# A graph network of two RGCN and two GAT layers on one core: unread products on TensorE before each slot's product

## The chip, the core and the metric

The kernel runs on one core of a Trainium2 chip. The time is the device time of one execution in microseconds. A core has TensorE (PE, matmuls from SBUF into PSUM banks), VectorE (DVE), ScalarE (ACT), GpSimd (POOL, which here issues all gathers) and SyncE (SP, DMA and semaphores). They run on their own and wait for each other by semaphores.

## The reference, cut to what matters

There are 6,250 nodes of 128 features and 100,000 edges, sorted by their destination `dst`. Two RGCN layers are followed by two GAT layers:

```
# RGCN, twice
agg = segment_sum(h[src], dst * 16 + rel)            # one sum per node and relation
out = relu(einsum('nri,rio->no', agg, W) + h @ loop_w + bias)
# GAT, twice, 4 heads
e     = leaky_relu(al_s[src] + al_d[dst], 0.2)
alpha = exp(e - segment_max(e, dst)[dst]) / segment_sum(...)[dst]
out   = segment_sum(alpha * xw[src], dst) + b
```

What costs is the sum over edges: a row per edge is gathered from a table in HBM and added to the row of its destination.

## The kernel before, in words

**Slots.** The edges lie in 784 tiles (`NT`) of 128 edges. The nodes lie in 49 windows of 128. A slot is a tile together with a window that it touches; there are 832 (`NS`). For each slot VectorE builds a 128 x 128 selection matrix `Sr` (1 where an edge's destination is a node of the window), TensorE multiplies it with the gathered tile `Gr` into a PSUM bank `B`, and VectorE adds the bank to the window's rows in `AC`. All of this is float32; TensorE takes such a product in two passes, so the profile shows two records for each.

**Stages.** After a first part (tables, layer norm, the table of the first RGCN layer) come four slot stages: RGCN layer 1 and 2 (`L` 0 and 1 in `tensor`, gathers on line 1872, slot products on line 1650, additions on line 852), and GAT layer 1 and 2 (`gat_tensor`, gathers on line 1889, slot products on line 1770, additions on line 1033). During the RGCN stages a turn (`onward_tensor`, `outward_tensor`) is woven in every 9 slots (`EVERY`): it takes a finished window, transposes it (line 1528, copied by VectorE on line 524) and multiplies it for the next layer (lines 1550 and 1552, or 1569). During the GAT stages `prep` is woven in: for the next chunk of 32 slots it transposes and multiplies in bf16 (lines 1705, 1719) and works out the weights of the edges with VectorE and ScalarE. The GAT chunks number 26.

**What orders the slots.** The order on each engine is written out by hand. The RGCN slot product waits for its bank, freed by the addition of three or four slots ago (`slot_add`; the banks are `RGCN_BANKS`, three in the first layer, four in the second), and for its tile: SyncE counts the landed gathers into `landed` (line 1914), and a register holds how many the slot needs. GpSimd gathers ahead, at most so far that tile `sn` waits for slot `sn - 16` (line 1871); in the GAT stages for slot `s - 96` (line 1888), and there a whole chunk's gathers are awaited by ScalarE in `prep`, not by TensorE. The GAT slot product waits for its bank alone (`gat_add`, three banks), and at a chunk's first slot for the weighing.

Of the kernel before, what the change touches and what calls it, by code (L numbers as in the profile page):

```python
# [37 lines left out]
HW = NW // 2  # L38
SLOW_STORES = (24, 30)
RGCN_BANKS = ((0, 1, 2), (0, 1, 2, 7))  # L40
PARAMS = 224
XC = 16
SG = 8
# [43 lines left out]
def build(nc, I, out, dbg=None):  # L87
# [7 lines left out]
    with ctx:  # L95
# [195 lines left out]
        def sel(s):  # L291
            return Sr[:, (s % SR) * P:(s % SR + 1) * P]
# [1262 lines left out]
        def outward_tensor(e, k):  # L1555
# [14 lines left out]
            yield  # L1570
            yield

        def tensor(e):
            pregs = [registers(e, f"t{k}", 16) for k in range(2)]
            kregs = [registers(e, f"tile{k}", 16) for k in range(2)]
            def mix(l, k):
                half, c = k // 2, k % 2
                if k == 0:
                    e.wait_ge(mixv.sem, mixv.at(f"wdg{l}"))
                    e.wait_ge(mix_par[l], 32)  # L1580
                if l:
                    e.wait_ge(mixa, 4 + k)
                e.matmul(B[7 if l else MIX_BANK[k]][:, :], wdg[l][:, half * P:(half + 1) * P], bas[l][:, c * 512:(c + 1) * 512],
                         start=True, stop=True).then_inc(mixp, 1)
            for k in range(4):
                mix(0, k)
            e.wait_ge(flagv.sem, flagv.at("sum"))
            e.wait_ge(const, CONST["ones"])
            e.matmul(B[1][0:1, 0:1], small[:, 0:1], ones[0:RF, 0:1], start=True, stop=True).then_inc(flagp, 1)

            tables = tables_tensor(e)
            early = False
            e.wait_ge(const, CONST["ident"])
            for w in range(-1, NW):
                if w + 1 < NW:
                    turned(e, w + 1)
                if w < 0:
                    continue
                e.wait_ge(hT_made, w + 1)
                for k in range(5):  # L1600
                    if w:
                        if k % 2 == 0 and k < 4:
                            e.wait_ge(row_a, 2 * (w - 1) + k // 2 + 1)
                        else:
                            e.wait_ge(row_v, 3 * (w - 1) + {1: 1, 3: 2, 4: 3}[k])
                    elif k == 0:
                        e.wait_ge(mixa, 4)
                        e.wait_ge(flagv.sem, flagv.at("flag"))
                    if k < 4:
                        if w == 0 and k == 0:  # L1610
                            e.wait_ge(wall_sem[0], 16)
                        e.matmul(B[k][:, :], hT[:, w % 2, :], wl[0][:, k * 512:(k + 1) * 512], start=True, stop=True).then_inc(row_mm, 1)  # L1612
                    else:
                        if w == 0:
                            e.wait_ge(first_params, 32)
                        e.matmul(B[k][:, 0:P], hT[:, w % 2, :], lw[0][:, :], start=True, stop=True).then_inc(row_mm, 1)
                if 8 <= w < 12:
                    if w == 8:
                        e.wait_ge(tv.sem, tv.at("rs"))
                    mix(1, w - 8)  # L1620
                if w >= 1 and not early:
                    early = next(tables) == "early"

            for L in range(2):
                turn = iter(())
                banks = RGCN_BANKS[L]

                def start(k):
                    return onward_tensor(e, k) if L == 0 else outward_tensor(e, k)
                if L == 0:  # L1630
                    e.wait_ge(params, PARAMS)
                    e.wait_ge(row_a, 2 * NW)
                    e.wait_ge(row_v, 3 * NW)
                    e.wait_ge(ta.sem, ta.at("oft1"))
                else:
                    e.wait_ge(rest_done, 1)
                for s in range(-LOOK, NS + LAG):
                    if 0 <= s < NS:
                        if s % 16 == 0:
                            e.reg_load(pregs[s % 32 // 16], OFT[0:1, s:s + 16])  # L1640
                            e.reg_load(kregs[s % 32 // 16], TIX[:, s:s + 16])

                        if s >= len(banks):
                            e.wait_ge(slot_add, L * NS + s - len(banks) + 1)
                        else:
                            e.wait_ge(built_v, L * NS + s + 1)

                        e.wait_ge(landed[L], kregs[s % 32 // 16][s % 16])
                        o = off(e, pregs[s % 32 // 16][s % 16], (TG - 1) * P)
                        e.matmul(B[banks[s % len(banks)]][:, 0:P], selr(s), Gr[:, bass.ds(o, P)], start=True, stop=True).then_inc(slot_mm, 1)  # L1650
                    sa = s - LAG
                    if sa >= 0:
                        if L == 0 and sa % 16 == 8:
                            next(tables, None)
                        k = (sa + 1 - FIRST) // EVERY
                        if sa + 1 >= FIRST and (sa + 1 - FIRST) % EVERY == 0 and k < NK:
                            finish(turn)
                            turn = start(k)
                    next(turn, None)
                finish(turn)  # L1660
                if L == 0:
                    finish(tables)
                turns = turns_of(NK, start)
                if L == 0:
                    for _ in range(2):
                        for x in turns:
                            next(x)
                    for x in turns:
                        finish(x)
                    rest(e, rest_tensor, "rt")  # L1670
                else:
                    for _ in zip(*turns):
                        pass
                    rest(e, rest2_tensor, "r2t")
            for L in range(2):
                gat_tensor(e, L, pregs)

        def gat_tensor(e, L, pregs):
# [79 lines left out]
            for c in range(NC):  # L1758
                gen = prep(c + 1) if c + 1 < NC else iter(())
                for i in range(CH):  # L1760
                    s = c * CH + i


                    if i == 0:
                        e.wait_ge(wei_v, L * (4 * NC - 3) + 4 * c + 1)
                    if c + 1 == NC and i in (8, 16, 24):
                        e.wait_ge(wei_g, 3 * L + i // 8)
                    if s >= 3:
                        e.wait_ge(gat_add, L * NS + s - 2)
                    e.matmul(B[s % 3][:, 0:CW], sel(s), Gr[:, (s % GR) * CW:(s % GR + 1) * CW], start=True, stop=True).then_inc(gat_mm, 1)  # L1770
                    if i < 12 or (i >= 14 and i % 2 == 0):
                        next(gen, None)
# [247 lines left out]
```

## Time and profile before

| | |
|---|---|
| median of 3 runs | 5546.97 us (5546.96 to 5551.64) |
| the profiled execution, its own time | 5593.81 us |
| its span in the trace | 5592.0 us |
| granted TensorE clock, mean | 0.604 |
| busy share of the span | PE 56%, weight loads 41%, DVE 46%, ACT 19%, POOL 57% |
| slot products | 1,664 on line 1650, 1,664 on line 1770, two records each |

A record of PE is one matmul pass; its start is measured, its end is modelled. PEclk is the clock that TensorE was granted, as a share of 2.4 GHz: 1.0 is 2.4 GHz and 0.5 is 1.2 GHz. An idle time is followed by an arrow and by what ended it; "issue" means nothing that the profile shows, "remote" a releaser that it could not name.

### The profile page before, as it was taken

How to read it: one execution, taken by the hardware profiler on the slowest of the kernel's cores; microseconds unless marked ns; L12 is line 12 of the kernel's file. 1: busy time of each engine (PE TensorE's matmuls, PEld its weight loads, DVE VectorE, ACT ScalarE, POOL GpSimd, SP SyncE). 2: the span in 40 equal slices, each digit the busy share in tenths (PEclk: the TensorE clock that was granted, in tenths of full speed). 3: DMA queues.
4: the chain of work that ended last, by engine and by line, in shares of the span. 5: the costliest groups of instructions: out<-in, count | busy, mean ns of one | idle time of the engine just before them, and what ended most of it. 6: DMA issues, size and time to landing. Idle time of an engine off the chain costs nothing.

```text
span 5592.0 us, 63654 instructions
## 1 busy us (share of the span) xinstructions
PE 3147.6 (56%) x12887; PEld 2272.1 (41%) x12887; DVE 2561.5 (46%) x9589; ACT 1064.3 (19%) x2505; POOL 3194.9 (57%) x3310
## 2 busy tenths in 40 slices
PE   7946666676734444444415555655651555555555
PEld 3434333343423333333314444444540444444444
DVE  6433333333333443444515555555571555555557
ACT  3301111121200000000102222222230222222223
POOL 0166666666266666666466666666526666666651
PEclk9957777777855555555555555555565555555556
DMA  6513333333322222222122222222102222222221
GB/s 238 228 44 111 124 121 118 118 119 123 115 71 53 55 54 54 55 54 56 35 48 45 45 45 45 45 45 45 39 26 49 46 44 45 45 45 45 45 43 47
DMA packets 168746, 395.78 MB, mean 71 GB/s; under 512 B 57590, under 2 KB 92468, under 8 KB 151092
## 3 DMA queue, kind: packets, MB, share of 16 engines
q0 software_dynamic: 103872, 215.70, 16.8%
q10 hardware_dynamic: 37968, 103.60, 4.8%
q1 hardware_dynamic: 26532, 72.39, 3.5%
q8 instruction: 126, 2.06, 0.2%
q14 instruction: 248, 2.03, 0.1%
HBM read 230.11 MB, written 161.35 MB: 70 GB/s over the span
## 4 chain that ended last, share of the span: by engine, by line
PE 34%; issue 22%; another core or an unknown queue 21%; DVE 13%; ACT 3%; POOL 2%; DVEq 2%; DMA 1%; SPq 1%; ACTq 0%; POOLq 0%
PE B L1770 9%; PE B L1650 8%; PE B L1550 6%; DVE AC L1033 3%; PE B L1612 3%; DVE AC L852 3%; PE B L1705 2%; PE B L1719 2%; ACT hold L1376 1%; POOL Gr L1889 1%; DVE Sr L937 1%; DVEq L308 1%; POOL Gr L1872 1%; DVE Sr L840 1%
## 5 line engine op out<-in xcount | busy, mean ns | idle before, releaser
L1889 POOL DMA_INDIRECT Gr<-Gtab,SRC x1664 | 1617.4, 972 | 1010.6 <-issue 471.4
L1872 POOL DMA_INDIRECT Gr<-Ttab,GID x1568 | 1501.8, 958 | 1045.6 <-issue 413.4
L1650 PE MATMUL B<-Gr,Sr 128*128 x3328 | 916.8, 402 | 723.7 <-issue 381.3
L1770 PE MATMUL B<-Gr,Sr 128*128 128x136 f32 x3328 | 1059.8, 462 | 402.2 <-DVE AC L1033 187.8
L1650 PEld LDWEIGHTS B<-Gr,Sr 128*128 128x128 f32 x3328 | 742.0, 279 | 1104.2 <-issue 1100.0
L1033 DVE TENSOR_TENSOR AC<-AC,B 128x136 f32 x1664 | 486.9, 293 | 1135.1 <-PE B L1770 470.8
L1770 PEld LDWEIGHTS B<-Gr,Sr 128*128 128x128 f32 x3328 | 786.4, 304 | 520.5 <-issue 243.6
L852 DVE TENSOR_TENSOR AC<-AC,B 128x128 f32 x1664 | 476.3, 286 | 937.8 <-remote 400.2
L1550 PE MATMUL B<-XW,hT 128*128 128x512 f32 x672 | 474.5, 798 | 90.3 <-ACT Sr L1202 32.9
L1705 PE MATMUL B<-identb,hold 128*128 128x128 bf16 x1664 | 251.9, 305 | 464.3 <-ACT hold L1376 259.5
L840 DVE TENSOR_SCALAR Sr<-iota,DL 128x128 f32<-128x128 f32 x1664 | 494.3, 299 | 15.8 <-issue 10.9
L1368 ACT CAST hold<-Sr 128x512 bf16<-128x512 f32 x416 | 257.6, 619 | 977.3 <-remote 500.1
L1705 PEld LDWEIGHTS B<-identb,hold 128*128 128x128 bf16 x1664 | 181.3, 138 | 524.5 <-ACT hold L1376 279.5
L937 DVE TENSOR_SCALAR Sr<-iota,DL 128x128 f32<-128x128 f32 x1664 | 373.8, 300 | 19.3 <-issue 18.9
L1202 ACT COPY Sr<-B 128x512 f32<-128x512 f32 x336 | 195.0, 585 | 648.2 <-PE B L1550 396.9
L1376 ACT COPY hold<-B 128x512 bf16<-128x512 bf16 x416 | 240.3, 584 | 147.7 <-PE B L1719 80.1
L1013 DVE TENSOR_TENSOR Gr<-Gr,B 128x1024 f32<-128x1024 f32 x202 | 245.2, 1214 | 3.4 <-issue 3.4
L1719 PE MATMUL B<-A,hold 128*128 x1664 | 163.2, 186 | 97.3 <-issue 44.4
L1719 PEld LDWEIGHTS B<-A,hold 128*128 128x128 bf16 x1664 | 148.1, 119 | 146.7 <-issue 131.7
L524 DVE COPY hT<-B 128x128 f32<-128x128 f32 x217 | 62.5, 289 | 309.2 <-remote 157.7
L1550 PEld LDWEIGHTS B<-XW,hT 128*128 128x128 f32 x672 | 136.8, 252 | 114.6 <-issue 41.7
L1612 PE MATMUL B<-XW,hT 128*128 128x512 f32 x392 | 179.0, 600 | 6.4 <-DVE hT L524 6.4
(275 smaller groups left out, 2358.2 us busy)
## 6 DMA issues: line engine op xcount, KB each, us to landing
Ttab<-Sr ACTq DMA_DIRECT2D x84, 1024.0 KB
Ttab<-Sr SPq DMA_DIRECT2D x51, 1024.0 KB
Gr<-Gtab,SRC POOLq DMA_INDIRECT x1664
Gr<-Ttab,GID POOLq DMA_INDIRECT x1568
Gtab<-Gr ACTq DMA_DIRECT2D x84, 66.0 KB
X1D<-Gr ACTq DMA_DIRECT2D x84, 64.0 KB
Gtab<-XW SPq DMA_DIRECT2D x7, 462.0 KB, 3.7
out<-Sr SPq DMA_DIRECT2D x12, 256.0 KB
```

What stands on the lines that cost most here:

```text
L840: e.tensor_scalar(out=selr(sn), in0=iota[:, :], scalar1=DL[:, sn:sn + 1], scalar2=None, op0=ALU.is_equal).then_inc(built_v, 1)
L852: e.tensor_tensor(a, a, B[RGCN_BANKS[L][sa % len(RGCN_BANKS[L])]][:, 0:P], ALU.add).then_inc(slot_add, 1)
L937: e.tensor_scalar(out=sel(s), in0=iota[:, :], scalar1=DL[:, s:s + 1], scalar2=None, op0=ALU.is_equal).then_inc(sel_made, 1)
L1033: e.tensor_tensor(a, a, B[s % 3][:, 0:CW], ALU.add).then_inc(gat_add, 1)
L1550: e.matmul(B[bk][:, :], hT[:, u % 2, :], wl[1][:, i * 512:(i + 1) * 512], start=True, stop=True).then_inc(row_mm, 1)
L1612: e.matmul(B[k][:, :], hT[:, w % 2, :], wl[0][:, k * 512:(k + 1) * 512], start=True, stop=True).then_inc(row_mm, 1)
L1650: e.matmul(B[banks[s % len(banks)]][:, 0:P], selr(s), Gr[:, bass.ds(o, P)], start=True, stop=True).then_inc(slot_mm, 1)
L1705: mm = e.transpose(bt[:, j * P:(j + 1) * P], sbf[:, g % 2, j * P:(j + 1) * P], identb[:, :])
L1719: mm = e.matmul(B[5][:, 12 * m:12 * m + 12], sts[:, g % 2, j * P:(j + 1) * P], A3[:, bass.ds(off(e, regs[m % 16], 12 * NW), 12)], start=Tr ...
L1770: e.matmul(B[s % 3][:, 0:CW], sel(s), Gr[:, (s % GR) * CW:(s % GR + 1) * CW], start=True, stop=True).then_inc(gat_mm, 1)
L1872: e.indirect_dma_start(out=Gr[:, (sn + 1) % TG * P:((sn + 1) % TG + 1) * P], out_offset=None, in_=Tt[L][:, :], in_offset=bass.IndirectOffs ...
L1889: e.indirect_dma_start(out=Gr[:, (s % GR) * CW:(s % GR) * CW + 132], out_offset=None, in_=T2[L][0:NPAD][:, :], in_offset=bass.IndirectOffs ...
```

## The change

Before each slot's product TensorE computes further products into the same bank: the bf16 identity as weight, the same identity read four times over as the moving side, so 128 x 512 elements of output. Nobody reads them, since the slot's product starts the bank anew. There is one for each slot of the first RGCN stage and three in the second, not in the last 40 slots (`CALM`), and two in both GAT stages, not in the last chunk. They stand behind the wait for the bank, and in the RGCN stages ahead of the wait for the tile. They signal nothing. The first RGCN stage also waits once for the constant `identb`.

```diff
+RGCN_BUSY, GAT_BUSY, CALM = (1, 3), 2, 40
...
+        def keep_busy(e, bank, n):
+
+            for _ in range(n):
+                e.matmul(B[bank][:, :].rearrange("p (k n) -> p k n", n=P), identb[:, :], identb[:, :].unsqueeze(1).to_broadcast([P, 4, P]),
+                         start=True, stop=True)
+
...
                 if L == 0:
+                    e.wait_ge(const, CONST["identb"])
                     e.wait_ge(params, PARAMS)
...
                             e.wait_ge(built_v, L * NS + s + 1)
+                        if s < NS - CALM:
+                            keep_busy(e, banks[s % len(banks)], RGCN_BUSY[L])
 
                         e.wait_ge(landed[L], kregs[s % 32 // 16][s % 16])
...
                     if s >= 3:
                         e.wait_ge(gat_add, L * NS + s - 2)
+                    if c + 1 < NC:
+                        keep_busy(e, s % 3, GAT_BUSY)
                     e.matmul(B[s % 3][:, 0:CW], sel(s), Gr[:, (s % GR) * CW:(s % GR + 1) * CW], start=True, stop=True).then_inc(gat_mm, 1)
```

On TensorE in the second RGCN stage, two slots stood like this before (L308 is the register instruction that carries the waits, L1650 the slot's product):

```order
L308 ISA [waits landed1,slot_added]
L1650 MATMUL B<-Gr,Sr 128x128
L1528 MATMUL B<-ident,hn 128x128 [waits hT_made,hn_made]
L308 ISA [waits landed1,slot_added]
L1650 MATMUL B<-Gr,Sr 128x128
```

and stand like this now (L1577 is the new product, L1660 the slot's, L309 the former L308, L1529 the former L1528):

```order
L1660 MATMUL B<-Gr,Sr 128x128
L1529 MATMUL B<-ident,hn 128x128 [waits hT_made,hn_made]
L1577 MATMUL B<-identb 128x512 [waits slot_added]
L1577 MATMUL B<-identb 128x512 x2
L309 ISA [waits landed1]
L1660 MATMUL B<-Gr,Sr 128x128
```

The wait for the bank has moved from the slot's own register instruction to the first of the three new products, and the wait for the tile stands behind all three.

On TensorE in the middle of a GAT chunk before (L1719 belongs to the preparation of the next chunk):

```order
L1719 MATMUL B<-A,hold 128x12
L1770 MATMUL B<-Gr,Sr 128x136 [waits gat_added]
L308 ISA [waits prep_scalar]
L1719 MATMUL B<-A,hold 128x12
L308 ISA
```

and now (L1729 is the former L1719, L1782 the former L1770):

```order
L1729 MATMUL B<-A,hold 128x12
L1577 MATMUL B<-identb 128x512 [waits gat_added]
L1577 MATMUL B<-identb 128x512
L1782 MATMUL B<-Gr,Sr 128x136
L309 ISA [waits prep_scalar]
L1729 MATMUL B<-A,hold 128x12
```

Two new products now stand between the preparation's products and the slot's, and they take over the wait for the bank.

## Rows read from the trace of the kernel before

**Rows 1.** The page: TensorE's granted clock in 40 slices, tenths of 2.4 GHz

```profile
PEclk9957777777855555555555555555565555555556
```

**Rows 2.** Stretches: length; busy (records) PE, PEld, DVE, ACT, POOL; clock, DMA share, GB/s

```profile
0.00:240.00 240.00, 204.51 (x607) 98.48 (x607) 136.63 (x384) 82.93 (x161) 19.93 (x40) 0.96 0.63 246
...
300.00:1440.00 1140.00, 750.38 (x2357) 450.65 (x2356) 414.05 (x1658) 198.20 (x380) 719.97 (x752) 0.74 0.34 112
1570.00:2700.00 1130.00, 505.02 (x1731) 394.15 (x1731) 452.03 (x2041) 85.01 (x298) 725.39 (x759) 0.53 0.21 53
2860.00:4030.00 1170.00, 658.54 (x3293) 530.35 (x3293) 587.44 (x2159) 263.69 (x646) 736.85 (x765) 0.53 0.20 45
4280.00:5440.00 1160.00, 658.53 (x3285) 530.71 (x3285) 587.23 (x2162) 261.55 (x642) 725.10 (x760) 0.53 0.21 45
1453.00:1523.00 70.00, 56.19 (x199) 33.30 (x199) 31.41 (x128) 18.55 (x35) 0.00 (x0) 0.85 0.24 99
2703.00:2752.00 49.00, 36.94 (x142) 30.20 (x141) 34.77 (x161) 7.53 (x26) 1.27 (x2) 0.57 0.13 24
5441.00:5523.00 82.00, 62.95 (x332) 51.36 (x332) 53.38 (x195) 21.64 (x54) 5.91 (x4) 0.67 0.02 2
```

**Rows 3.** The additions alone in those stretches, L852 then L1033 (x counts slots)

```profile
300.00:1440.00 1140.00, 215.18 (x750) 0.74 0.34 112
1570.00:2700.00 1130.00, 216.47 (x758) 0.53 0.21 53
...
1453.00:1523.00 70.00, 17.68 (x62) 0.85 0.24 99
2703.00:2752.00 49.00, 17.02 (x60) 0.57 0.13 24
...
4280.00:5440.00 1160.00, 215.21 (x736) 0.53 0.21 45
...
5441.00:5523.00 82.00, 27.01 (x92) 0.67 0.02 2
```

**Rows 4.** Timeline of 16 us in RGCN layer 2: start, us, what

```profile
1858.70 0.28 PE L1528 MATMUL B<-ident,hn 128*128 128x128 f32 x1
...
1859.76 0.95 POOL L1872 DMA_INDIRECT Gr<-Ttab,GID  x1 [0.30 <-issue]
...
1872.09 0.29 DVE L524 COPY hT<-B 128x128 f32<-128x128 f32 x1 [11.24 <-remote]
1872.44 0.82 PE L1569 MATMUL B<-wx,hT 128*128 128x136 f32 x2 [13.11 <-DVE hT L524]
```

**Rows 5.** Gather lines L1872, then L1889: what ended GpSimd's idle time

```profile
  remote: 223.6, 109
  PE B L1650: 211.9, 221
...
  PE B L1770: 248.5, 255
  remote: 230.9, 104
```

**Rows 6.** RGCN slot products: durations (min/median/max), and idle ended by SyncE

```profile
L1650 PE MATMUL B<-Gr,Sr x3328: 272/421/583, 263.9 to 2751.7; 128*128 x196
...
  SPq L1914: 48.6, 12
```

**Rows 7.** Timeline at a change of clock, end of GAT layer 2

```profile
5472.90 0.50 PE L1770 MATMUL B<-Gr,Sr 128*128 128x136 f32 x2 [0.46 <-DVE AC L1033]
5473.35 0.40 PE L1705 MATMUL B<-identb,hold 128*128 128x128 bf16 x4
5474.52 0.82 PE L1770 MATMUL B<-Gr,Sr 128*128 128x136 f32 x2 [0.78 <-DVE AC L1033]
5475.13 0.63 PE L1705 MATMUL B<-identb,hold 128*128 128x128 bf16 x4
```

**Rows 8.** The bf16 transposes of GAT layer 2

```profile
L1705 PE MATMUL B<-identb,hold x732: 216/314/314, 4295.5 to 5437.2; 128*128 128x128 bf16 x183
```

## The prediction

> **What bounds the kernel now.** I read the page first. TensorE's matmuls are busy for 56% of the span and GpSimd for 57% (the table of the profile above), neither of them full, and the line of granted clocks stands at 5 tenths from the 15th slice on, against 9 at the start [rows 1]. So from about 1,560 us on TensorE runs at 1.2 GHz, and this is what the change aims at.
>
> Next the table of stretches, cut where the four slot stages are in steady state (gathers running) and where their gathers have ended [rows 2], and the same stretches for the two lines of VectorE that add one slot each, which count the slots [rows 3]. Dividing gives us per slot. First RGCN stage: 1140/750 = 1.52. Second: 1130/758 = 1.49. The GAT stages: 1170/736 = 1.59 and 1160/736 = 1.58 (736 in both). In the tails without gathers the same work takes 70/62 = 1.13, 49/60 = 0.82 and, at the end of the last stage, 82/92 = 0.89; I take the GAT layer before it for the same.
>
> Is it the gathers, then, that set the pace? Each takes GpSimd 0.95 us and 0.30 us of issue, 1.26 us from start to start [rows 4], less than 1.49 to 1.59. GpSimd itself waits, and for TensorE: the two gather lines waited 212 + 249 us for the slot products and 224 + 231 us for releasers without a name, which at these lines can only be earlier slots or earlier gathers; 915 us in all [rows 5]. Seen from TensorE, the wait for a landed tile (SyncE's line 1914) ended only 49 us of idle time before the RGCN slot products [rows 6]. Tiles are there early; TensorE is late. That is the first warning for this change: the time in which TensorE waits **for a tile** is next to nothing.
>
> What is TensorE late with? By the stretches its matmuls are busy 1.00, 0.67, 0.89 and 0.89 us per slot, and the rest is 0.52, 0.82, 0.70 and 0.68 us. In the tails the rest is only 0.22 (1.13 - 56.19/62), 0.20 and 0.21 us. The timeline shows what the rest is made of: products that have been issued and are taken note of much later. A transpose (L1528) of 0.28 us starts at 1858.70, the copy that waits for it starts at 1872.09, and in these 13 us TensorE starts nothing, while gathers go on every 1.26 us [rows 4]. I call such a stretch a hold. The trace does not tell what makes one; it shows that they are long where gathers run and TensorE is sparse, and nearly absent in the tails.
>
> **The change part by part.** (1) One wait for `identb` before the first RGCN stage. The first slot product starts at 264 us [rows 6], long after GpSimd has made its constants: nothing.
>
> (2) Products: 792 slots x 1, 792 x 3, and 2 x 25 chunks x 32 slots x 2 = 3,200; 6,368 in all. No row shows this product, so it is bounded. It streams 512 bf16 columns over a bf16 weight, as many as four of L1705's. A train of four of these took 0.63 us in the cold clock and 0.40 in the warm one [rows 7]; one alone lasts up to 0.31 and at least 0.22 [rows 8]. So start to start (0.63 - 0.31)/3 = 0.107 and (0.40 - 0.22)/3 = 0.06, and a product is 0.43 us cold and 0.24 warm. The upper bounds are the trains themselves, 0.63 and 0.40. I take 0.43 and 0.24.
>
> (3) The clock. In the second RGCN stage at 1.2 GHz the work would be 0.67 + 3 x 0.43 = 1.96 us per slot, more than the 1.49 that a slot has: TensorE would have no idle time. In the first 240 us, where it is busy for 204, the granted clock is 0.96 [rows 2]. So the clock will rise to 2.4 GHz. For the GAT stages 0.89 + 0.86 = 1.75 against 1.58 says the same, and so does 1.00 + 0.43 or less against 1.52 for the first stage, whose clock is 0.74 already. What warm clocks save: a slot's pair took 0.82 us cold and 0.50 warm [rows 7]. For the busy time per slot, full scaling by the granted clock is the low bound (0.74, 0.35, 0.47, 0.47) and today's value the high one. Latency in each record doesn't scale, as the pair shows (0.50/0.82 = 0.6, not 0.5), so I take 0.74, 0.42, 0.55 and 0.55. With the products: 0.98, 1.14, 1.03 and 1.03 us.
>
> (4) What happens to the rest (0.52 to 0.82) decides the sign, and no row gives it. Low bound: the tails' 0.20 to 0.22. High bound: unchanged. Since the rest is smallest where TensorE is densest (0.52 at 1.00 busy, 0.82 at 0.67), and since a product behind a slot leaves fewer moments without work on TensorE, I take the middle: 0.37, 0.51, 0.45, 0.44 (the GAT stages' with 0.21). Then a slot takes 1.35, 1.65, 1.48, 1.47 us; against now -0.17, +0.16, -0.11, -0.11. The sum: 792 x (-0.17 + 0.16) + 800 x (-0.11 - 0.11) = -8 - 176 = **-184 us**.
>
> What is queued behind: each product stands before its slot's product and waits for the same free bank, so it also stands in front of the turn products and of the preparation of the next chunk (L1705, L1719), for whose results ScalarE and VectorE wait. Tails keep their present order (`CALM`, last chunk), so they cost nothing. GpSimd, VectorE and ScalarE get no new instruction.
>
> In the timeline nothing that TensorE has to do passes the product that is held [rows 4]. By the Trainium skill ("TensorE: Matmul & The Clock Gate", Part 3) matmuls start and end strictly in program order and only weight loads are pulled ahead. By that rule no product can be passed by a slot whose tile is there, so that each one's whole length lands on the slot's path; this trace agrees, and it is the first rival's mechanism.
>
> **How it stands to the median.** The profiled execution took 5593.8 us (span 5592.0), the median of the runs is 5547.0. The difference is 0.8%, and I take the -184 us over unchanged: 5547 - 184 = 5363, about **5360 us**.
>
> **Rivals.**
> - *Slower: the holds stay, and the products are added work on the engine that is late.* For it: GpSimd waits for TensorE and not the other way round [rows 5, 6]; the hold of [rows 4] came over a product that had already been started. Rest unchanged: 0.98 + 0.52 = 1.50, 1.14 + 0.82 = 1.96, 1.03 + 0.70 = 1.73, 1.03 + 0.68 = 1.71: 792 x (-0.02 + 0.47) + 800 x (0.14 + 0.13) = +572 us, 6120. Place: the slot's product of the second RGCN stage above all. It decides as soon as the rest falls by less than 572/3184 = 0.18 us per slot. Against it: the rest is not fixed; it is 0.30 smaller in the denser first stage, and it has no reason to hold still.
> - *Much faster: the holds go altogether.* Then rests of 0.22, 0.20, 0.21, 0.21 give 1.20, 1.34, 1.24, 1.24, and the gathers' 1.26 becomes the bound in three stages: 792 x (-0.26 - 0.15) + 800 x (-0.33 - 0.32) = -845 us, 4700. For it: the tails. Against it: tails have no gathers, and it may be these that make the holds. Part of it reaches to 5100.
> - *No change.* The pace with gathers is nearly the same in stages of very different load (1.49 to 1.59 for 0.67 to 1.00 busy), so something near 1.5 us may be set by gathers and holds together, and warm clock and products cancel: 5547, give or take 11.
>
> **How the numbers follow.** Forecast (5100 to 5536): 0.45. Much faster (4700 to 5100): 0.20. No change (within 0.2% of 5547, 11 us, about what a measurement of this kernel can tell): 0.07. Slower (from 5558 to 6120): 0.28. Faster is 0.45 + 0.20 = 0.65, same 0.07, slower 0.28. The range leaves out the lower part of the much-faster case (0.07 below 4950) and the upper half of the slower one (0.13 above 5720): 4950 to 5720. The likeliest case by itself spans 5200 to 5500.
>
> **What would show it.** Step 3: granted clock over 0.9 in the stretches of all four stages, the slot pair near 0.50 us, weight loads of L1650 near 0.19 us instead of 0.33. Step 2: the products' line with 6,368 pairs, starts 0.22 to 0.24 us apart. Step 4: us per slot of each stretch, and GpSimd's 915 us of waiting for TensorE: some 700 left if I am right, nearly none for the second rival, more than now for the first. I expect the GAT stages to give most, and the second RGCN stage, with three products, to give nothing or lose. The prediction is wrong if the clock stays at 5 tenths, or if the rest per slot doesn't move, or if it falls to that of the tails.

## The result and the profile after

The changed kernel takes 5660.36 us (median of 4 runs, 5656.65 to 5661.23), the kernel before 5546.97 us (4 runs beside it, 5545.41 to 5551.64): a ratio of 1.0197, 95% interval 1.0185 to 1.0210. It is 2.0% slower, where I had forecast 3.4% faster. The profiled execution has a span of 5659.5 us, against 5592.0 before.

The page of the kernel after: granted clock, and the top of the chain that ended last.

```profile
PEclk8969888898888889888758788888875888888787
...
PE 54%; issue 16%; another core or an unknown queue 14%; DVE 10%; ACT 3%; DVEq 1%; DMA 1%; SPq 1%; POOL 1%; ACTq 0%; POOLq 0%
PE B L1577 23%; PE B L1782 7%; PE B L1660 7%; PE B L1551 6%; PE B L1619 3%; PE B L1729 2%; DVE AC L853 2%; PE B L1715 2%; DVE AC L1034 2%; ACT hold L1377 1%; DVE Sr L938 1%; PE B L1529 1%; DMA Gr<-Ttab,GID 1%; DVEq L309 1%
```

The clock did what the change aims at [against rows 1], and the unread products (line 1577) are the largest item of the chain, 23%. The stretches of the kernel after, columns as in [rows 2]:

```profile
300.00:1440.00 1140.00, 800.68 (x3096) 498.27 (x3096) 410.74 (x1654) 197.79 (x380) 720.12 (x750) 0.85 0.34 111
1575.00:2725.00 1150.00, 836.01 (x4007) 531.71 (x4006) 453.01 (x2038) 84.56 (x297) 725.55 (x757) 0.88 0.21 53
2895.00:4075.00 1180.00, 811.33 (x4737) 574.92 (x4737) 582.81 (x2139) 261.66 (x642) 737.85 (x762) 0.80 0.20 45
4330.00:5500.00 1170.00, 806.78 (x4727) 571.43 (x4728) 582.57 (x2136) 261.93 (x642) 724.81 (x755) 0.80 0.20 45
```

And the additions in them, as in [rows 3] (line 853 in the RGCN stages, 1034 in the GAT stages):

```profile
300.00:1440.00 1140.00, 214.33 (x748) 0.85 0.34 111
1575.00:2725.00 1150.00, 216.31 (x758) 0.88 0.21 53
...
2895.00:4075.00 1180.00, 214.03 (x732) 0.80 0.20 45
4330.00:5500.00 1170.00, 214.16 (x730) 0.80 0.20 45
```

Dividing gives the comparison. Rest is the part of a slot in which TensorE isn't busy.

| per slot, us | RGCN 1 | RGCN 2 | GAT 1 | GAT 2 |
|---|---|---|---|---|
| pace before, after | 1.52, 1.52 | 1.49, 1.52 | 1.59, 1.61 | 1.58, 1.60 |
| busy before, after | 1.00, 1.07 | 0.67, 1.10 | 0.89, 1.11 | 0.89, 1.11 |
| rest before, after | 0.52, 0.45 | 0.82, 0.41 | 0.70, 0.50 | 0.68, 0.50 |
| clock before, after | 0.74, 0.85 | 0.53, 0.88 | 0.53, 0.80 | 0.53, 0.80 |

TensorE's busy time grew by 0.07 to 0.43 us and its rest shrank by nearly as much: the pace hardly moved. GpSimd's gather lines wait a little longer than in [rows 5], 973 us in all against 915; these 58 us are most of what the span grew by:

```profile
POOL Gr L1901 <- PE B L1782: 294.9, 322, 3.3
POOL Gr L1884 <- PE B L1660: 271.0, 267, 4.3
POOL Gr L1901 <- remote: 226.9, 113, 11.3
POOL Gr L1884 <- remote: 180.1, 95, 4.1
```

From its first to its last addition a stage now takes 1263, 1226, 1280 and 1280 us, against 1258, 1199, 1265 and 1262: +5, +27, +15 and +18, in sum 65 of the 67.5 us by which the span grew. (The profiled execution of before was 47 us above its median, that of after near it; hence 113 us between the medians.)

Where TensorE has slots waiting, it does them flat out. Its timeline in RGCN layer 2:

```profile
2002.22 0.38 PE L1660 MATMUL B<-Gr,Sr 128*128 x2
2002.44 0.81 PE L1577 MATMUL B<-identb 128*128 128x512 bf16 x3
2003.09 0.39 PE L1660 MATMUL B<-Gr,Sr 128*128 x2
2003.31 0.81 PE L1577 MATMUL B<-identb 128*128 128x512 bf16 x3
```

A slot every 0.87 us, of which the three products take 0.65 (2003.96, the next slot's product, less 2003.31; 0.217 us from start to start).

### The profile page after: what moved, and what is told of

The parts are those of the page before. It is cut to its first block, busy times and chain, and to the rows that moved or that the text cites. A ratio compares the mean times of both kernels' runs of the same rounds, so it can differ in the third digit from the quotient of the medians.

```text
span 5659.5 us, 74806 instructions
## 1 busy us (share of the span) xinstructions
PE 3885.0 (69%) x19255; PEld 2561.7 (45%) x19255; DVE 2561.3 (45%) x9589; ACT 1064.5 (19%) x2505; POOL 3206.8 (57%) x3310
## 4 chain that ended last, share of the span: by engine, by line
PE 54%; issue 16%; another core or an unknown queue 14%; DVE 10%; ACT 3%; DVEq 1%; DMA 1%; SPq 1%; POOL 1%; ACTq 0%; POOLq 0%
PE B L1577 23%; PE B L1782 7%; PE B L1660 7%; PE B L1551 6%; PE B L1619 3%; PE B L1729 2%; DVE AC L853 2%; PE B L1715 2%; DVE AC L1034 2%; ACT hold L1377 1%; DVE Sr L938 1%; PE B L1529 1%; DMA Gr<-Ttab,GID 1%; DVEq L309 1%
## 5 line engine op out<-in xcount | busy, mean ns | idle before, releaser
L1577 PE MATMUL B<-identb 128*128 128x512 bf16 x6368 | 2212.9, 434 | 769.5 <-issue 343.9
L1577 PEld LDWEIGHTS B<-identb 128*128 128x128 bf16 x6368 | 595.6, 106 | 1157.0 <-issue 525.8
L1782 PEld LDWEIGHTS B<-Gr,Sr 128*128 128x128 f32 x3328 | 746.5, 226 | 334.2 <-issue 115.7
L1660 PEld LDWEIGHTS B<-Gr,Sr 128*128 128x128 f32 x3328 | 705.4, 218 | 339.6 <-issue 203.3
L1782 PE MATMUL B<-Gr,Sr 128*128 128x136 f32 x3328 | 762.7, 318 | 5.7 <-DVE AC L1034 4.6
L1660 PE MATMUL B<-Gr,Sr 128*128 x3328 | 721.6, 304 | 25.1 <-DVE AC L853 11.4
L1551 PE MATMUL B<-XW,hT 128*128 128x512 f32 x672 | 414.8, 705 | 120.3 <-issue 70.8
L1715 PE MATMUL B<-identb,hold 128*128 128x128 bf16 x1664 | 198.9, 255 | 260.5 <-ACT hold L1377 122.1
L1715 PEld LDWEIGHTS B<-identb,hold 128*128 128x128 bf16 x1664 | 153.4, 117 | 289.9 <-ACT hold L1377 133.2
L1729 PE MATMUL B<-A,hold 128*128 x1664 | 154.7, 177 | 83.0 <-ACT hold L1377 49.1
L1619 PE MATMUL B<-XW,hT 128*128 128x512 f32 x392 | 182.8, 610 | 7.2 <-DMA XW<-Wrel 5.3
```

The source lines that it names most:

```text
L1551: e.matmul(B[bk][:, :], hT[:, u % 2, :], wl[1][:, i * 512:(i + 1) * 512], start=True, stop=True).then_inc(row_mm, 1)
L1577: e.matmul(B[bank][:, :].rearrange("p (k n) -> p k n", n=P), identb[:, :], identb[:, :].unsqueeze(1).to_broadcast([P, 4, P]), start=True, ...
L1715: mm = e.transpose(bt[:, j * P:(j + 1) * P], sbf[:, g % 2, j * P:(j + 1) * P], identb[:, :])
```

## Experiments

The kernels that are timed against each other ran in sets, one chip for each set, with the kernel before beside them. It took 5543.5 us on the chip of the e1 runs, 5615.5 (e2), 5601.8 (e3), 5606.9 (e4), and 4651.9 us on that of the d runs, so compare within a set. The ratio is to the kernel before in the same set. Stage times are from the first to the last addition of a stage in the trace; "-" is the same code as in the kernel before, so its time is a control.

| run | ratio [95%] | RGCN 1 | RGCN 2 | GAT 1 | GAT 2 |
|---|---|---|---|---|---|
| e1_control | 1.0009 [1.0000, 1.0018] | 1244 - | 1186 - | 1251 - | 1254 - |
| e1_after | 1.0225 [1.0212, 1.0239] | 1263 | 1229 | 1275 | 1272 |
| e1_r2_only | 1.0084 [1.0070, 1.0098] | 1245 - | 1229 | 1254 - | 1252 - |
| e1_gat_only | 1.0108 [1.0092, 1.0123] | 1239 - | 1189 - | 1281 | 1282 |
| e2_ones | 1.0138 [1.0122, 1.0153] | 1297 | 1223 | 1285 | 1288 |
| e2_r2_six | 1.0319 [1.0305, 1.0333] | 1299 | 1295 | 1304 | 1300 |
| e2_no_gathers | 0.9018 [0.9005, 0.9030] | 1262 - | 658 | 1263 - | 1270 - |
| e2_no_gathers_after | 0.9391 [0.9378, 0.9404] | 1286 | 772 | 1298 | 1294 |
| e3_narrow | 1.0195 [1.0178, 1.0212] | 1282 | 1241 | 1287 | 1290 |
| e3_shallow | 1.0041 [1.0026, 1.0056] | 1256 - | 1218 | 1266 - | 1264 - |
| e3_after | 1.0234 [1.0217, 1.0250] | 1284 | 1249 | 1296 | 1296 |
| e4_tight | 0.9934 [0.9921, 0.9947] | 1255 | 1200 | 1250 | 1253 |
| e4_pause | 0.9886 [0.9872, 0.9900] | 1244 | 1197 | 1261 | 1256 |
| e4_pause_after | 1.0295 [1.0281, 1.0308] | 1290 | 1267 | 1310 | 1316 |
| d_ones | 1.0172 [1.0155, 1.0189] | 1050 | 1023 | 1046 | 1037 |
| d_shallow | 1.0181 [1.0160, 1.0201] | 1052 | 1030 | 1044 | 1036 |
| d_none | 0.9319 [0.9301, 0.9338] | 1050 | 632 | 1044 | 1036 |
| d_plain | 0.8806 [0.8789, 0.8824] | 1048 | 632 | 1041 | 820 |

All kernels of the e runs carry one register operation more per slot; e1_control is the kernel before with this alone, and I call it the control:

```diff
+            need = e.alloc_register("tiles_needed")
...
-                        e.wait_ge(landed[L], kregs[s % 32 // 16][s % 16])
+                        e.reg_alu(need, kregs[s % 32 // 16][s % 16], 1, op=mybir.AluOpType.max)
+                        e.wait_ge(landed[L], need)
```

**d_ones, d_shallow, d_none, d_plain: a chip without holds.** They wait for the tile by a constant instead:

```diff
-                        e.wait_ge(landed[L], kregs[s % 32 // 16][s % 16])
+                        e.wait_ge(landed[L], min(s + 1, NT))
```

that is for up to 48 tiles more than a slot needs. The kernel before with this wait alone (c_control), and three more with it, gave no time, so its cost wasn't measured. An estimate from the trace of d_ones: in the two RGCN layers 55 and 51 slots are left behind the last gather and take 63 and 45 us, which could cover the 79 us by which d_ones is slower than the kernel before. d_ones has one product per slot in every stage (`RGCN_BUSY, GAT_BUSY, CALM = (1, 1), 1, 40`). d_shallow has two banks in RGCN layer 2:

```diff
-RGCN_BANKS = ((0, 1, 2), (0, 1, 2, 7))
+RGCN_BANKS = ((0, 1, 2), (0, 1))
```

d_none leaves out the gathers of RGCN layer 2 (its slots multiply what lies in SBUF), and d_plain replaces those and the gathers of GAT layer 2 by plain loads of as many rows, from GpSimd's queue too. The sums of these layers aren't the reference's.

> The changed kernel on the control with one product per slot in every stage. Work: in the second RGCN stage at most 0.43 us cold or 0.22 warm is added per slot and the clock stays low for part of the time; total 5540 to 5640. Signals: products fit into idle time, and what the clock gives back is kept: 5480 to 5580.

> Control with two banks in place of four for the slots of the second RGCN stage. Signals: how far TensorE can run ahead of the news is the number of banks, so two make the stage markedly longer, 1350 to 1700 us in place of 1199. Work: TensorE is held by itself, banks are rarely what it waits for, 1199 to 1260.

> Control in which the second RGCN layer gathers nothing: GpSimd counts up a semaphore in place of each gather and the slots multiply the tiles that lie there (the computation leaves out that layer's gathers). Every theory in which gathers cause the holds: 832 slots at the tail's 0.82 us, 680 us in place of 1199, and TensorE's gaps over 3 us gone. If the holds come from the order of waits among TensorE, VectorE and ScalarE itself: over 1000 us.

> Control in which the gathers of the second layer of each kind are plain loads by GpSimd's queue: the same 128 rows of 512 or 528 bytes into the same place, but rows that follow on each other, so the result is not the reference's (the computation leaves out the gathering there). Both stages keep their order and waits. If GpSimd's making of descriptors is what holds TensorE's news back: the second RGCN stage falls from 1199 us to that of its tail, 832 x 0.82 = 680 to 800 us, likewise the second GAT stage from 1262 to 740 to 850. If it is the traffic into SBUF: both stay above 1100.

These expectations go by the times of the comparison's chip, so d_ones and d_shallow missed them by far. The surprise was the kernel before itself: 4651.9 us, 895 less than in the comparison, nearly the 915 us that GpSimd waited in [rows 5] there. In d_ones those waits are gone; each is the 0.3 us between two gathers:

```profile
POOL Gr L1884 <- issue: 305.3, 1001, 0.3
POOL Gr L1884 <- PE B L1660: 172.3, 565, 0.3
POOL Gr L1901 <- PE B L1782: 122.3, 401, 0.3
```

Its timeline shows the cadence:

```profile
2003.15 0.96 POOL L1884 DMA_INDIRECT Gr<-Ttab,GID  x1 [0.30 <-issue]
2004.42 0.95 POOL L1884 DMA_INDIRECT Gr<-Ttab,GID  x1 [0.30 <-issue]
```

Gathers start every 1.263 us. A GAT stage has 832 of them, which make 1051 us, about its time. An RGCN stage has only 784, one for each tile: 990 us, and then the slots behind the last gather. e2_ones, with the same products, takes 1297, 1223, 1285 and 1288 us on its chip. So gathers allow 1.26 us per slot in a GAT stage and 1.19 in an RGCN stage. What lies above that on the other chips I put down to the holds of [rows 4]; in what else the chips differ isn't known. Even here TensorE and VectorE both stand still for over 2 us 22 times in 720 slots of each GAT stage, once in a chunk, where ScalarE waits for the chunk's gathers. Without gathers RGCN layer 2 takes 632 us, 0.76 per slot, with plain loads in their place no more, and GAT layer 2 with plain loads 820.

**e1: the parts, on a chip with holds.**

> The kernel before, with one register operation per slot ahead of TensorE's wait for its tile (the number of tiles waited for is the same); every other run of this set carries it too, and is compared with this one. Both theories: 1.000 of the kernel before, within 0.2%. If the extra operation costs TensorE 50 ns in each of 3,200 slots and none is hidden, up to 160 us.

> The changed kernel with the same register operation. Two theories. PACE: the chip's pace of a slot is set by GpSimd's gathers and by how soon TensorE's news arrives, TensorE's load only fills the time between; the products then cost 0 to 2% wherever the run is made: on a chip on which the kernel before takes about 5547 us, 5660 (1.020); on one on which it takes about 4652 us, 1.00 to 1.02. CLOCK (my forecast's rival, the extra busy time is on the path): the time grows with the products' busy time, +0.05 to 0.4 us a slot, so on the fast kind of chip, where the pace of 1.25 us a slot lies nearer to the busy 1.1 us, the loss must be larger, 1.03 or more.

e1_r2_only is the changed kernel with `RGCN_BUSY, GAT_BUSY, CALM = (0, 3), 0, 40`, e1_gat_only with `(0, 0), 2, 40`.

> Three products per slot in the second RGCN layer alone (800 slots), none elsewhere. By the traces of before and after that layer went from 1199 to 1226 us on the chip of the comparison, so PACE gives +27 us (1.005) there, and 0 where the pace is GpSimd's 1.25 us. My forecast of step 4 gave a gain of 70 to 180 us for this layer, whose rest per slot was largest.

> Two products per slot in both GAT layers alone. By the traces the two went from 2527 to 2560 us, so PACE gives +33 us (1.006) on the chip of the comparison, and 0 where the pace is GpSimd's. If parts add, this run and the one before it sum with the first layer's +5 to the whole change's +65.

The register operation costs nothing that can be told (3 us, interval 0 to 10). e1_after repeats the result (5665.4 us). The parts add up: by medians +42 (RGCN layer 2), +57 (GAT), and by its stage +19 (RGCN layer 1) make 118 of the 118.5 us. In the table each dose costs in its own stage, and the stages without one keep their time within 5 us. No part gains. (The forecast had RGCN layer 2 lose 0.16 us per slot, 127 us; the gain of 70 to 180 us that the expectation of e1_r2_only names is not what step 4 said.)

How each stage loses is seen in the intervals between additions of the middle 720 slots. In RGCN layer 2 the median, the pace of catching up, goes from 0.71 us (control) to 0.95 (e1_after), while the intervals over 5 us go from 253 us in sum to 140. In the GAT stages it goes from 1.03 and 1.06 to 1.31, and the long ones from 193 and 165 us to 27 and 46. So the products do shorten holds, and slow down what follows them.

**e2: dose, and the cover taken away.** e2_ones has `(1, 1), 1, 40`, e2_r2_six `(1, 6), 2, 40`.

> One product per slot in all four stages (with the register operation of the control). Two theories. TRADE: the products shorten the longest holds, and lengthen every slot of the catching up behind a hold by their own 0.22 us; both go with their number. Then a third of the products in the second RGCN layer and half in the GAT layers cost a third and a half: +18 (first RGCN layer, unchanged dose) +14 +15 +14 = +61 us, 1.011. WARM: one product is enough to hold the clock at 2.4 GHz, which shortens the holds as three do, and costs only a third: then the second RGCN layer gains (its interval between additions when catching up goes from 0.71 us to no more than 0.8), and the whole is 1.000 or less.

> As the changed kernel, but with six products per slot in the second RGCN layer instead of three. TRADE: catching up goes from 0.95 us per slot to 0.95 + 3 x 0.217 = 1.60, more than a gather's 1.26, so TensorE is the bound there: 792 x 1.60 + 40 x 0.8 = 1300 us instead of 1229, the whole 5735 (1.035). If the products only fill what the holds leave: as with three, 1.022.

e2_no_gathers is the control and e2_no_gathers_after the changed kernel, both without the gathers of RGCN layer 2 (whoever waited for a gather waits for the count `left_out`), whose sums are then not the reference's:

```diff
+                    if L == 1:
+                        e.sem_inc(left_out, 1)
+                        continue
                     e.indirect_dma_start(
```

> The control with the gathers of the second RGCN layer left out (its slots multiply what lies in SBUF; the output isn't the reference's). If the gathers make the holds: that layer takes 0.76 us per slot, 632 us instead of 1186, with next to no gap of TensorE over 3 us, the whole 4990 (0.90). If holds come from TensorE and its news alone: over 0.9 us per slot, gaps of 3 us and more in it.

> The changed kernel, gathers of the second RGCN layer left out likewise. Beside the run before it this shows what three products cost per slot where no gather covers them. TRADE: the slot goes from 0.76 us to about 0.95, the interval of the catching up (2.4 GHz gives back part of 3 x 0.217), +150 us in that layer, and the whole +150 + 18 + 54 = +220 us on the run before it. If the products were free in TensorE's idle time: +70.

For RGCN layer 2 on this chip I take 1186 x 1.012 = 1200 us as the time without products (the control's stages, scaled by the unchanged ones of e2_no_gathers: 1262/1244, 1263/1251, 1270/1254). One product costs 23 us there, three 43 (e1), six 95. That is some 0.03, 0.05 and 0.12 us per slot for 0.22, 0.65 and 1.3 us of TensorE: dear for nothing gained, but a tenth of what it would be on the path all the time. Such a price is good to some 10 us: in RGCN layer 1 one product costs 19 us in e1, and 24, 35 and 37 in the three runs of e2 that have it. Six give 1295 us, where TRADE said 1300, and TensorE is full. e2_ones came out near TRADE's 1.011; WARM's 1.000 is out. The layer's window in e2_r2_six, then in e2_no_gathers and e2_no_gathers_after:

```profile
1600.00:2700.00 1100.00, 1075.65 (x5709) 635.22 (x5707) 415.98 (x1839) 75.23 (x264) 667.03 (x693) 1.00 0.20 51
```

```profile
1570.00:2180.00 610.00, 456.22 (x1760) 371.62 (x1758) 447.81 (x2066) 87.70 (x308) 0.00 (x0) 0.61 0.06 18
```

```profile
1600.00:2320.00 720.00, 698.76 (x4076) 483.39 (x4075) 455.00 (x2076) 87.81 (x308) 0.00 (x0) 1.00 0.05 16
```

Without gathers there is no hold: not one gap of TensorE over 3 us in 720 slots, where the control of e1 has 68, and 0.79 us per slot against 1.43. So the holds come with the gathers. Whether they come with GpSimd's work on them or with their traffic isn't told apart: plain loads in their place ran only on the chip without holds. Three products then cost 114 us (150 were expected), with TensorE busy for 97% of the window at full clock.

**e3: what has a price?** e3_narrow has the doses of the change with products of 128 columns, e3_shallow the two banks of above, e3_after is e1_after again.

```diff
-                e.matmul(B[bank][:, :].rearrange("p (k n) -> p k n", n=P), identb[:, :], identb[:, :].unsqueeze(1).to_broadcast([P, 4, P]),
-                         start=True, stop=True)
+                e.matmul(B[bank][:, 0:P], identb[:, :], identb[:, :], start=True, stop=True)
```

> As the changed kernel (one, three and two products per slot), but each product streams 128 columns, not 512. Now a product should take some 0.06 us of TensorE instead of 0.22 (the train of four of 128 columns took 0.40 us, one alone 0.22). TRADE: the cost goes with the columns, a quarter of the changed kernel's +120 us, and what the clock gives comes on top: the clock rises to 0.65 at least in the second RGCN layer, 0.995 to 1.005 of the kernel before. If the price is one of instructions (each matmul costs its place in the queue whatever it streams) and not of columns: as the changed kernel, 1.02. If the warmer clock alone were worth what my forecast said: 0.97 or less.

> The control with two banks instead of four for the second RGCN layer's slots: TensorE may run two slots ahead of VectorE's additions and no more. If late news between TensorE and VectorE is what stretches the slots, this layer grows by 100 us or more (1.02 or more) on a chip with holds. If only the catching up of TensorE itself counts: under 30 us, 1.005 or less.

> The changed kernel again (with the control's register operation), on the chip of the two runs before it, as their measure. Both theories: 1.020 to 1.023 where the kernel before takes about 5550 to 5620 us. On a chip where it takes about 4650 us, where holds are absent and the pace is GpSimd's 1.25 us a slot: TRADE says 1.000 to 1.003 in sum, since catching up at 0.95 (second RGCN layer) is hidden, with the GAT layers' 1.31 us a slot just above the pace: up to +0.05 x 1600 = 80 us, 1.017.

Products of a quarter of the columns (0.056 or 0.107 us from start to start, by the clock) cost 1.95% against 2.34%, not the quarter that TRADE expected. The clock rises less, to 0.63 in RGCN layer 2. But the pace of catching up is nearly as slow as with wide ones, 0.88 us there and 1.24 and 1.27 in the GAT stages (e3_after: 0.95 and 1.31). So the price doesn't go with the columns. Nor does it go with that pace alone: two banks make it as slow, 0.96, and cost 20 us in that layer (against 1186 x 1.010 = 1198; under the 30 that the expectation gives to TensorE's own catching up), the wide products 51; and one wide product (e2_ones) also catches up at 0.88 and costs 23, three narrow ones 43. The rival that the expectation of e3_narrow names, a price for each product whatever it streams, fits best: one costs 23, three 43 to 51, narrow or wide. It isn't proven, because the narrow products also left the clock lower, so the slots' own matmuls took longer.

**e4: does GpSimd's pause end the silence?** In the control's trace there are stretches over 2 us in which neither TensorE nor VectorE does anything, 80 of them in the middle 720 slots of RGCN layer 2, 317 us in all. One of them, in which ScalarE runs for 0.2 us:

```profile
2015.11 0.79 PE L1652 MATMUL B<-Gr,Sr 128*128 x2 [0.23 <-issue]
...
2015.40 0.28 DVE L840 TENSOR_SCALAR Sr<-iota,DL 128x128 f32<-128x128 f32 x1
2016.40 0.96 POOL L1874 DMA_INDIRECT Gr<-Ttab,GID  x1 [0.30 <-issue]
2016.57 0.20 ACT L1223 ACTIVATE rstd<-rstd 128x1 f32<-128x1 f32 x1 [5.56 <-DVE rstd L716]
2017.67 0.96 POOL L1874 DMA_INDIRECT Gr<-Ttab,GID  x1 [0.30 <-issue]
2018.93 0.96 POOL L1874 DMA_INDIRECT Gr<-Ttab,GID  x1 [0.31 <-issue]
2020.18 0.29 DVE L852 TENSOR_TENSOR AC<-AC,B 128x128 f32 x1 [4.50 <-issue]
...
2020.70 0.79 PE L1652 MATMUL B<-Gr,Sr 128*128 x2 [4.80 <-issue]
2020.81 0.95 POOL L1874 DMA_INDIRECT Gr<-Ttab,GID  x1 [0.92 <-issue]
```

Every product that had been started is done by 2015.90, yet VectorE's next addition starts at 2020.18: 0.3 us after the gather of 2018.93 ends, in a moment in which GpSimd issues none (the next one comes 0.6 us later than its cadence). Of the 80 silences 55 (69%) end in a pause of GpSimd (0.5 us or more without a gather) or within 1 us behind it, and such moments make up 25% of the stage. That is a correlation only; the next two kernels make such pauses. e4_tight lets GpSimd run less far ahead, e4_pause makes it wait before every eighth gather for the gather just before:

```diff
-                    back = sn - TG + NS - NT
+                    back = sn - 8
...
-                    if s >= GR:
-                        e.wait_ge(gat_mm, L * NS + s - GR + 1)
+                    if s >= GR - 16:
+                        e.wait_ge(gat_mm, L * NS + s - GR + 17)
```

```diff
+                    if sn % 8 == 7:
+                        wait_gather(e, n - 1)
                     back = sn - TG + NS - NT
...
                     wait_gather(e, n - NSG)
+                    if s % 8 == 7:
+                        wait_gather(e, n - 1)
                     if s >= GR:
```

> The control, with GpSimd held closer to TensorE: an RGCN gather may be 8 slots ahead of TensorE's slot products, not 16 and more, a GAT gather 80 slots, not 96. Theory PAUSE: news between engines is late while gathers follow each other without a break, and the silence ends when GpSimd has to stop for TensorE; the chip finds its own pace, whatever TensorE's load. Then an earlier stop makes silences shorter (fewer than half of the 80 silences over 2 us of TensorE and VectorE in the second RGCN layer left) and the time changes little, 0.99 to 1.01. Theory TRADE alone (holds come from elsewhere, GpSimd's pauses only follow): silences stay, GpSimd stops more often and the RGCN stages lose, 1.02 or more.

> The control, with a pause of GpSimd before every eighth gather: it waits until the gather just before has landed (about 1 to 2 us instead of the 0.30 us between gathers). PAUSE: silences over 2 us nearly go in all stages, the late gathers (150 to 180 us per stage) are replaced by 100 pauses of about 1.5 us, 150 us per stage: 0.98 to 1.01. Rival (pauses don't end silences): both add, 4 x 150 us, 1.10.

> The changed kernel with the same pauses. If pauses end the silences, TensorE's load has nothing left to shorten, and the products cost or cover what they do on their own: second RGCN layer 1.08 busy under a pace of 1.4: within 0.5% of e4_pause. If the products' price is the catching up behind a silence (TRADE) it goes away with the silences as well. If they lengthen TensorE's chain in any case: 2% above e4_pause, as without pauses.

Both made the kernel faster, by waits added to the engine that issues all gathers: 0.9934, and 5547.8 us against 5606.9, 0.9886. They beat both kernels. What ended VectorE's idle time in RGCN layer 2, control and then e4_pause:

```profile
DVE AC L852 <- remote: 241.5, 71, 6.6
DVE hT L524 <- remote: 140.7, 25, 10.1
```

```profile
DVE AC L852 <- PE B L1652: 243.3, 208, 3.4
DVE AC L852 <- issue: 139.5, 159, 3.2
DVE hT L524 <- issue: 128.9, 49, 4.4
...
DVE AC L852 <- remote: 0.4, 1, 0.4
```

The 382 us of waits without a visible releaser, up to 10.1 us long, are gone, though VectorE's seven largest groups of waits in the window still come to 611 us, against 623. The silences over 2 us in that layer fell from 80 to 11, from 317 to 25 us. In sum the deliberate pauses took the place of the late gathers: 86 intervals between gathers over 1.36 us, 179 us in excess of 1.255, against 98 and 150 in the control of e1. In RGCN layer 1 silences fell too (32 to 21); in the GAT stages they rose (32 and 29 to 56 and 59), yet these don't take longer.

Of the 59 us gained 33 show in the four stages (control scaled by 1.011: 1258, 1200, 1265, 1268), and only 3 of them in RGCN layer 2, where the silences went. Another 14 lie outside the stages (594 us against 608 in the control): the first addition of each GAT stage comes 7 us sooner after its first gather. So fewer silences didn't by themselves make a stage shorter. What the traces do show is where the time went. RGCN layer 2, gathers and additions, control and then e4_pause (first and last start):

```profile
L1874 POOL DMA_INDIRECT Gr<-Ttab,GID x784: 950/958/1049, 1529.1 to 2677.2; - x196
L852 DVE TENSOR_TENSOR AC<-AC,B x832: 272/286/319, 1540.9 to 2726.5; 128x128 f32 x167
```

```profile
L1876 POOL DMA_INDIRECT Gr<-Ttab,GID x784: 952/958/1031, 1527.9 to 2731.5; - x196
L852 DVE TENSOR_TENSOR AC<-AC,B x832: 273/286/318, 1539.4 to 2736.1; 128x128 f32 x167
```

The same for every stage: us from the first to the last gather; slots whose addition comes after the last gather; us that they take.

| run | RGCN 1 | RGCN 2 | GAT 1 | GAT 2 |
|---|---|---|---|---|
| e1_control | 1173; 64; 75 | 1148; 62; 49 | 1254; 93; 79 | 1254; 93; 80 |
| e4_tight | 1196; 56; 63 | 1168; 57; 44 | 1269; 78; 63 | 1267; 80; 66 |
| e4_pause | 1241; 2; 6 | 1204; 3; 5 | 1298; 49; 39 | 1289; 49; 39 |
| e4_pause_after | 1230; 55; 64 | 1226; 63; 53 | 1311; 90; 75 | 1308; 91; 80 |

In the control GpSimd is about as far ahead as it may be when it issues its last gather, and 62 to 93 slots are still to do. With the pauses the gathers take longer, not shorter, by 21 to 55 us (control scaled: 1186, 1161, 1268, 1268), but few slots are left behind them, and the end of a stage shrinks by 40 to 69 us. That is the gain in the stages. e4_tight left the silences in RGCN layer 2 (76), so my "fewer than half left" was wrong, and gained in the GAT stages, 30 of its 38 us: there its gathers take as long as the scaled control's, and the end is shorter by 16 and 14 us.

e4_pause_after went against what I expected: 4.1% above e4_pause, not within 0.5%. With the products the pauses don't help: 41 silences in RGCN layer 2, as many as in e1_after (42), 109 late gathers, and all four stages are the longest of the set. TensorE is again 55 to 91 slots behind at the last gather, so the gathers are longer and the ends hardly shorter. The products cost 229 us beside pauses and 113 to 130 without.

## Why the prediction was wrong

- **Step 1**, the wait for `identb`: nothing, as forecast.
- **Step 2**, 6,368 products of 0.24 us warm: right; 0.217 us from start to start.
- **Step 3**, the clock and the busy time: in part. The clock rose to 0.80 to 0.88, not over 0.9, and warm matmuls gave back less: without the products' 0.217 us each, TensorE's busy time fell to 0.85, 0.45, 0.67 and 0.67 us per slot, where I took 0.74, 0.42, 0.55 and 0.55 (for the first stage my own low bound). With the products busy came to 1.07, 1.10, 1.11, 1.11 against 0.98, 1.14, 1.03, 1.03. By the sum's own weights that is 792 x (0.09 - 0.04) + 800 x (0.08 + 0.08) = +168 us.
- **Step 4**, the rest: "I take the middle", 0.37, 0.51, 0.45, 0.44. It fell to 0.45, 0.41, 0.50, 0.50: 792 x (0.08 - 0.10) + 800 x (0.05 + 0.06) = +72 us. Together 240 us, which takes -184 to +56, near the 65 us of the traces.
- **The step that failed is the sum in step 4**, busy plus rest, as if each were a quantity of its own: the busy term missed by 168 us, the rest by 72. The runs show instead that the rest is what a pace made elsewhere leaves. In e1 to e3, chips with holds, the middle 720 slots of a stage with gathers take 1.48 to 1.59 us each, for busy times from 0.66 (e1_control) to 1.56 (e2_r2_six, where TensorE is full and no rest is left); the gathers alone would allow 1.19 or 1.26 (d runs). The kernel before had said so: 1.49 to 1.59 for 0.67 to 1.00, the ground of my *No change* rival, which I gave 0.07. That row deserved most of the chance. That 5660 us lies within my 4950 to 5720 is no credit to the mechanism; it got there from the other side.
- The *slower* rival has the sign but not the mechanism: its rest unchanged, 6120 us. The rest fell by 0.07 to 0.41. *Much faster* held that holds would go altogether; with the products the longest go, but TensorE's gaps over 2 us in RGCN layer 2 only fall from 101 to 58 (e1_control, e1_after). And its bound of 1.26 us per slot holds for the GAT stages alone, since an RGCN layer has 784 gathers for 832 slots.
- The warning that a product stands before its slot's product was right where TensorE is behind: catching up went from 0.71 to 0.95 and from 1.03 to 1.31 us per slot. In the GAT stages that is more than a gather's 1.26, at which no backlog can be worked off while gathers go on; but the control doesn't work it off either (93 slots left behind its last gather, 96 in e1_after). Nor does each product's whole length land on the slot's path, as the prediction took from the order of the matmuls: per slot it is 0.03 to 0.12 us for 0.22 to 1.3 us of products with gathers, and 0.14 for 0.65 without. The Trainium skill ("TensorE: Matmul & The Clock Gate", Why this matters for your kernels) advises to avoid idle gaps between bursts of matmuls, lest the clock fall. This trace agrees as to the clock, 0.53 to 0.88; the time went the other way.

**What stays open.** Why news is late while gathers run back to back, on some chips and not on others. By what path a product costs GpSimd and the slots their 20 to 50 us in a layer, nearly the same for 128 columns and for 512, and more than twice what two banks cost at the same pace of catching up. Why TensorE falls behind again when products and pauses come together. What the whole change does on the chip without holds wasn't measured; d_ones there had the same stage times as d_shallow within 7 us, so one product per slot costs next to nothing where gathers alone set the pace.

## What to carry to other kernels

When stages of very different load run at one pace, that pace is made elsewhere; find what makes it before pricing work on the engine that seems late, and don't add a busy and an idle estimate as if they were independent. Filling an engine's idle time to raise its clock can pay only if its own work was the limit, and no run here shows it paying; clocks of 0.53 and 0.88 gave nearly the same pace, and the filler cost on every chip with holds. Look at what is left to do when a stage's last gather is issued: an engine that streams far ahead leaves the whole backlog for the end. One short pause per eight gathers took 1.1% off here, by a shorter end and not by a faster stream; with the products on TensorE the same pauses gained nothing.

## What the runs showed of the hardware

- The same kernel takes 4651.9 us on one chip and 5543.5 to 5615.5 us on four others (and 5547 in the comparison). On the first (d_ones), 3 intervals between the gathers of 720 slots of RGCN layer 1 are over 1.36 us; on the others 148 to 186 are, in the kernels without pauses.
- On those, news between TensorE, VectorE, ScalarE and GpSimd can come late by 4 to 13 us while gathers follow each other every 1.26 us ([rows 4], e1_control); with the gathers of RGCN layer 2 left out (e2_no_gathers) TensorE has no gap over 3 us in 720 slots.
- A bf16 product of 128 columns streams in 0.056 us from start to start at 2.4 GHz and 0.107 at 1.2, one of 512 columns in 0.217 at 2.4.
